# A transformer layer with attention and routed experts: routing and scatters moved among the first maxima, the sorted tiles closer together

## What is computed

```python
xn = _layernorm(x, axis=-1)                      # x: 8 x 256 x 128
x = x + attn(xn, Wqkv, bqkv, Wout, bout) + ffn(xn, ...)
# attn: 16 heads of 8 with rotary q and k
scores = jnp.einsum('bhtd,bhsd->bhts', q, k) / math.sqrt(D)
attn = jnp.einsum('bhts,bhsd->bhtd', jax.nn.softmax(scores, axis=-1), v)
# ffn: one shared expert, and the best 2 of 16
router_logits = jax.nn.sigmoid(x @ gate_w + gate_b)
expert_values, expert_indices = jax.lax.top_k(router_logits, k=2)
expert_values = expert_values / jnp.sum(expert_values, axis=-1, keepdims=True)
hg = jnp.einsum('bsd,edi->bsei', x, experts_wg)  # 128 -> 64
hu = jnp.einsum('bsd,edi->bsei', x, experts_wu)
all_outputs = jnp.einsum('bsei,eid->bsed', jax.nn.silu(hg) * hu, experts_wd)
# the two chosen, weighted; plus x and the shared expert
```

## Time and profile before

| | us |
|---|---|
| median of 3 runs | 302.07 (299.94 to 302.34) |
| the profiled execution, whole | 301.69 |
| its span, from first to last instruction | 299.9 |
| PE busy, share of the span | 213.9 (71%) |
| DVE busy | 150.9 (50%) |
| POOL busy | 143.9 (48%) |
| ACT busy | 127.6 (43%) |
| mean granted clock of PE | 0.869 of full speed |

### The profile page before, as it was taken

How to read it: one execution, slowest core, us unless ns; L and a number is a source line. 1 busy time by engine, 2 the same in 40 slices (tenths; PEclk the granted TensorE clock), 3 DMA queues, 4 the chain that set the end, 5 groups by cost and what they waited for, 6 DMA issues and landing times.

```text
span 299.9 us, 4752 instructions
## 1 busy us (share of the span) xinstructions
PE 213.9 (71%) x1603; PEld 131.2 (44%) x1603; DVE 150.9 (50%) x374; ACT 127.6 (43%) x292; POOL 143.9 (48%) x160
## 2 busy tenths in 40 slices
PE   0758965376868999139778789786978999996300
PEld 0326821162635545027545557474754446442200
DVE  6670199915494888213544365423526887710100
ACT  1365100002634676204544557644466776675000
POOL 9581048961347777780003370000000588888882
PEclk9995596757897999859999999979999999999555
DMA  7317689920325433152624142731225353333233
GB/s 254 52 39 209 179 213 271 276 83 0 107 72 152 111 107 108 52 136 72 183 82 109 43 117 74 205 97 37 87 77 156 97 97 41 39 39 70 36 70 87
DMA packets 50913, 32.48 MB, mean 108 GB/s; under 512 B 4542, under 2 KB 48830, under 8 KB 50622
## 3 DMA queue, kind: packets, MB, share of 16 engines
q1 hardware_dynamic: 43178, 26.40, 32.3%
q0 software_dynamic: 5632, 4.21, 8.0%
q10 hardware_dynamic: 2080, 1.57, 1.8%
HBM read 16.21 MB, written 15.77 MB: 107 GB/s over the span
## 4 chain that ended last, share of the span: by engine, by line
PE 42%; POOL 18%; issue 13%; ACT 8%; DVE 8%; DMA 7%; POOLq 1%; SPq 1%; ACTq 0%; DVEq 0%
POOL x_sorted L1054 10%; POOL resid L1071 8%; PE PV L600 7%; DMA q_hat<-mT 5%; PE S2a L586 4%; PE S2b L586 3%; PE Fa L515 2%; PE S1a L572 2%; PE Fc L483 2%; DVE mx L975 2%; PE S1b L572 2%; ACT ys L675 2%; PE Fb L467 2%; PE Fb L528 2%; PE Fa L528 2%
## 5 line engine op out<-in xcount | busy, mean ns | idle before, releaser
L1071 POOL DMA_INDIRECT resid<-y_sorted,slot_of x32 | 49.4, 1545 | 66.0 <-DMA y_sorted<-ys 56.5
L740 ACT ACTIVATE probs<-S2a 128x512 f32<-128x512 f32 x64 | 38.1, 596 | 62.8 <-PE S2a L586 62.6
L975 DVE TENSOR_REDUCE mx<-S1a 128x2 f32<-128x512 f32 x64 | 44.0, 687 | 41.5 <-PE S1a L572 40.9
L740 ACT ACTIVATE probs<-S2b 128x512 f32<-128x512 f32 x64 | 38.3, 598 | 49.2 <-PE S2b L586 48.8
L975 DVE TENSOR_REDUCE mx<-S1b 128x2 f32<-128x512 f32 x64 | 44.0, 688 | 8.9 <-PE S1b L572 8.2
L600 PE MATMUL PV<-probs,vx 128*32 128x256 f32 x512 | 41.6, 398 | 1.1 <-ACT probs L740 1.0
L586 PE MATMUL S2a<-q_hat,k_hat 102*128 102x256 bf16 x128 | 25.7, 283 | 19.7 <-DMA q_hat<-mT 18.6
L1054 POOL DMA_INDIRECT x_sorted<-xw,slot_of x32 | 31.8, 995 | 9.9 <-issue 8.5
L323 POOL TENSOR_TENSOR rope<-rope 128x256 f32<-128x256 f32 x14 | 10.2, 732 | 42.7 <-DVE rope L902 42.6
L572 PE MATMUL S1b<-k_hat,q_hat 96*128 96x256 bf16 x128 | 25.5, 281 | 5.2 <-DVE mx L975 5.2
L572 PE MATMUL S1a<-k_hat,q_hat 96*128 96x256 bf16 x128 | 26.2, 288 | 4.1 <-DVE mx L975 4.1
(11 more groups left out here) (197 smaller groups left out, 370.9 us busy)
## 6 DMA issues: line engine op xcount, KB each, us to landing
x_sorted<-ys SPq DMA_DIRECT2D x1, 3096.0 KB, 23.0
xs<-x_sorted SPq DMA_DIRECT2D x12, 258.0 KB, 3.1
q_hat<-q_parts SPq DMA_DIRECT2D x32, 96.0 KB, 2.3
y_sorted<-ys SPq DMA_DIRECT2D x12, 256.0 KB, 2.4
k_hat<-k_parts SPq DMA_DIRECT2D x28, 96.0 KB, 2.5
q_parts<-parts SPq DMA_DIRECT2D x8, 192.0 KB, 2.4
k_parts<-parts SPq DMA_DIRECT2D x7, 192.0 KB, 2.2
wgu_sb<-in_wgu SPq DMA_DIRECT2D x1, 1088.0 KB, 9.4
```

Source lines behind the costliest of these rows:

```text
L740: nc.scalar.activation(probs[:, head % (2 * NQ), :], S2[head % 2][:], ACT.Exp, scale=SCALE).then_inc(exp_done, 1)
L975: nc.vector.tensor_reduce(mx[:, (q // QB) % 2, (q // 2) % 2, :, q % 2, i], S1[i % 2][:].rearrange("p (t s) -> p t s", t=SB), axis=AX.X, op ...
L1071: nc.gpsimd.indirect_dma_start(resid[:, g, at, :], None, ys_dram, bass.IndirectOffsetOnAxis(ap=slot_of[:, t, k:k + 1], axis=0), compute_op ...
```

## The change

Seven edits, all in order and place but the last two:

- **Prologue.** `xw` of groups 1 to 3 on ACT, and DVE's variances for them, stand behind the split of batch 0. The zero fill of `x_sorted` goes from SP's queue to ACT's, as soon as group 0 has been loaded; `wgu`, `wd`, `wout` and `bout` go to ACT's queue behind V0.
- **Routing** starts at step -14 and does two stages a step, RANK stands in step -7, placement in steps -5 to -2, and POOL issues four scatters a block from block -1.
- **POOL.** Half-splits are set into other blocks (group 1, slot 1 into 2; group 2 into 5 and 10). `residual` goes from blocks -4, -1, 0, 1 to 11, 12, 13, 16. Group 2 is projected in blocks 2 and 3.
- **Sorted groups.** T of group `j` in step 46 + 5j//2, U two steps later, H seven, D ten. The buffer of loaded groups has seven places. The gathers stand from block 20 and still wait for all stores.
- **ACT** reads a step's items ahead of its exponential.
- **PE** loads a group's four register values with T, not with U.
- **Weights.** POOL multiplies the hidden values by the row's weight (`weigh`, in step 3 of a group); H waits for it. ACT's eviction of D is one plain copy.

```diff
-FIRST_SHARED, FIRST_SPARSE = 0, 10
-XRING = 6
+FIRST_SHARED, FIRST_SPARSE = 0, 46
+XRING = 7
...
-RESIDUAL_BLOCK = {-4: 0, -1: 1, 0: 2, 1: 3}
+RESIDUAL_BLOCK = {11: 0, 12: 1, 13: 2, 16: 3}
...
-ROUTE_STEP = -12
-PLACE_STEP = 1
-SORTED_LEAD, STORED_LAG = 6, 9
-SCATTER_BLOCK = 2
-SCATTERS = 5
-GATHER_BLOCK = 21
+ROUTE_STEP = -14
+PLACE_STEP = -5
+SORTED_LEAD, STORED_LAG = 5, 12
+SCATTER_BLOCK = -1
+SCATTERS = 4
+GATHER_BLOCK = 20
...
-        for kind, late in (("T", 0), ("U", 2), ("H", 5), ("D", 7)):
+        for kind, late in (("T", 0), ("U", 2), ("H", 7), ("D", 10)):
...
                 elif kind == "H":
-                    emptied(pe, ("U", n))
+                    if n < G:
+                        emptied(pe, ("U", n))
+                    else:
+                        pe.wait_ge(hid_weighed, n - G + 1)
...
+            act.wait_ge(ld_x[0], 16)
+            act.wait_ge(ys_zeroed, 1)
+            act.dma_start(xs_dram.rearrange("(p j) c -> p (j c)", p=P).rearrange("p (j c) -> p j c", c=ZERO),
...
-                    for t in range(QT):
-                        last = nc.scalar.activation(ys[:, j % OUTS, t, :], bank[:, t * C:(t + 1) * C], ACT.Copy,
-                                                    scale=xs[:, j % XRING, t, C:XW])
-                    last.then_inc(done, 1)
+                    nc.scalar.activation(ys[:, j % OUTS].rearrange("p t c -> p (t c)"), bank[:], ACT.Copy).then_inc(done, 1)
...
-                if 0 <= blk < NBLK:
-                    exponentials(blk * NQ + i)
...
                 for kind, n in items_before(blk, i):
                     read(kind, n)
+                if 0 <= blk < NBLK:
+                    exponentials(blk * NQ + i)
...
+            def weigh(j):
+
+                emptied(pool, ("U", G + j))
+                rows = hid[:, (G + j) % 2].rearrange("p (t i) -> p t i", i=I)
+                nc.gpsimd.tensor_tensor(rows, rows, xs[:, j % XRING, :, C:XW].broadcast_to([P, QT, I]),
+                                        ALU.mult).then_inc(hid_weighed, 1)
```

More of the change, by code:

```diff
@@ L496, in fill @@
                     j = n - G
+                    if j == 0:
+                        pe.wait_ge(owner_ready, 1)
+                    _, owners[n] = nc.values_load_multi_w_load_instructions(
+                        owner_at[0:1, QT * j:QT * (j + 1)], engines=[mybir.EngineType.PE], min_val=0, max_val=(E - 1) * P,
+                        skip_runtime_bounds_check_because="it is the least of a count and 15, times 128")
                     pe.wait_ge(xs_ld[j % XRING], 16 * (j // XRING + 1))
@@ L505, in fill @@
                     else:
-                        if n == G:
-                            pe.wait_ge(owner_ready, 1)
                         emptied(pe, ("T", n))
-                        _, owners[n] = nc.values_load_multi_w_load_instructions(
-                            owner_at[0:1, QT * (n - G):QT * (n - G + 1)], engines=[mybir.EngineType.PE],
-                            min_val=0, max_val=(E - 1) * P,
-                            skip_runtime_bounds_check_because="it is the least of a count and 15, times 128")
                         tiles, at = xsT[:, n % 2], owners[n]
@@ L715, in _ @@
                     act.dma_start(dram, parted).then_inc(scratch_done[0], 16)
-            read("X", 1)
-            normalise(3)
-            read("X", 2)
-            read("X", 3)
+            act.wait_ge(stats_ready, 2)
+            nc.scalar.activation(std[:, 1:], veps[:, 1:], ACT.Sqrt).then_inc(std_ready, 1)
+            for g in range(1, G):
+                normalise(g)
+            for g in range(1, G):
+                read("X", g)
             act.wait_ge(scratch_done[0], 16 * WRITES)
@@ L727, in _ @@
             read("V", 0)
+            act.dma_start(wgu_sb[:], wgu).then_inc(ld_up, 16)
+            act.wait_ge(wd_zeroed, 1)
+            for z in range(2):
+                act.dma_start(wd_sb[z][I * z:I * (z + 1), :], wd).then_inc(ld_down, 16)
+            act.dma_start(wout_sb[:], wout).then_inc(ld_wout, 16)
+            act.dma_start(bout_sb[:], bout.broadcast_to([P, C])).then_inc(ld_wout, 16)
             def halve_shared():
@@ L979, in _ @@
                     split_maxima(h, stage + 1)
[L980 to L983 removed]
+                for stage in range(ROUTE_STAGES):
+                    if ROUTE_STEP + stage // 2 == at:
+                        route(stage)
+                for stage in range(PLACE_STAGES):
+                    if PLACE_STEP + stage // 2 == at:
+                        place_rows(stage)
             for kind, n in EPILOGUE:
@@ L1076, in _ @@
                 split_batch(w, 0, 1)
-            for blk in range(FIRST, LAST + 1):
-                for (g, w, slot), at in SPLIT_BLOCK.items():
-                    if blk == at:
-                        split_batch(w, g, slot)
-                if blk in RESIDUAL_BLOCK:
-                    residual(RESIDUAL_BLOCK[blk])
-                first = SCATTERS * (blk - SCATTER_BLOCK)
-                for n in range(max(first, 0), min(first + SCATTERS, TOPK * NT)):
-                    scatter(n)
-                first = GATHERS * (blk - GATHER_BLOCK)
-                for p, k in gather_order()[max(first, 0):max(first + GATHERS, 0)]:
-                    gather(p, k)
+            for blk, i in steps():
+                if i == 0:
+                    for (g, w, slot), at in SPLIT_BLOCK.items():
+                        if blk == at:
+                            split_batch(w, g, slot)
+                    if blk in RESIDUAL_BLOCK:
+                        residual(RESIDUAL_BLOCK[blk])
+                    first = SCATTERS * (blk - SCATTER_BLOCK)
+                    for n in range(max(first, 0), min(first + SCATTERS, TOPK * NT)):
+                        scatter(n)
+                    first = GATHERS * (blk - GATHER_BLOCK)
+                    for p, k in gather_order()[max(first, 0):max(first + GATHERS, 0)]:
+                        gather(p, k)
+                for j in range(QUADS):
+                    if sparse_step(j) + 3 == 4 * blk + i:
+                        weigh(j)
     return nc
```

45 lines of the change are left out of this document (15 added, 30 removed), and 4 rows, old and new, of the table SPLIT_BLOCK.

## The result

The changed kernel takes 274.8 us (median of four, 274.3 to 275.31) where the kernel before takes 302.2 on the same chip: a ratio of 0.910 (95%: 0.903 to 0.916). I had said 287 and a range of 277 to 297.

A forecast was written before the change was run, and what follows sets the result against it. The run of gathers on POOL, waiting for the last sorted tile, ends the chain. First T at 135, 81.4 us to the last D, 4.1 to the first gather, then 64.4: 284.9, stated as 287 us; range 277 to 297.

The forecast's parts named there:

- The frame: End of the kernel: the time is when the last sorted tile is stored plus 64.4 us, gathers unchanged.
- the prologue's 5.3: Ahead of the first maximum: xw and variances now stand behind batch 0's split, making the prologue 5.3 us later.
- POOL's chain: POOL from the slots at 66.0: scatters 42.9, half-splits 19.2, first residual 2.5, ending at 130.6 and setting the pace.
- the new wait of DVE for the first residual: Step 42: DVE waits some 5 us for POOL's residual(0) before reading O1 of batch 1.
- the sorted stage: First T to last D: 75.7 us of PE work at 0.93 full, 81.4 us, ending at 216.4.
- The work: PE's work from first T to last D: 80.4, minus 2.8 for three steps, minus 1.9 for O1: 75.7 us.
- The fill: How full PE is in the sorted groups: 0.93, between 0.83 as before and 0.99 as without sorted tiles.
- My sum for the front: Steps ahead of the first T: step 0 at 68, then 54.9 us adjusted; step 42 at about 125 without POOL's wait.
- Rival 1: Front or sorted groups: prologue not late, 281.5 us, or PE at 0.99, 282; both 277. Chance 0.2.
- Rival 2: Sorted groups stay loose: fills bunched on three banks, PE 0.83, 90.9 us, 296.5 as a whole. Chance 0.22.
- Rival 3: Whole kernel: hardly any gain, 299 to 305; sorted groups loose and another 3 to 8 us lost in front. Chance 0.08.
- Rival 4: Sorted groups: H waits for POOL's multiplication, each group losing 1.5 us or more, time over 305. Chance 0.05.

The follow-up runs named there:

- the old front: The kernel before with ACT reading items first and the changed kernel's sorted stage; prologue, zero fill, routing, scatters, half-splits and residuals as before: 272.03 us, ratio 0.909.

## Why the prediction was right, and where it failed

- **The frame held.** "When the last tile is stored, plus 64.4": 64.3 to 64.5 us in every kernel timed. The span from last D to first gather was 4.1 by my sum and 3.8 in the trace.
- **Everything on the path up to the first T held** within 2 us: the prologue's 5.3 (5.0 at the first maximum; 4.1 there and 5.0 at the first T against the run with the old one), the slots, POOL's chain (64.5 us from the slots to the residual, 64.6 by my sum), and the new wait of DVE for the first residual, which the run with early residuals confirmed as on the path. That the first T stands within 0.2 us of 135 is luck: the residual came 1.5 us early, and T followed 5.7 us behind it where I had taken some 4.
- **The step that failed is the sorted stage, in both of its terms.** I wrote "PE's work: 80.4, minus three steps of 0.93 (2.8), minus O1 (1.9): 75.7", and then a fill of 0.93. The busy time was 69.2 and the fill 0.98. With the right busy time alone my sum gives 74.4 us, so 7.0 of the 10.9 us missed are work and 3.9 are fill.
- **The work.** The mis-sized term is the 80.4 from which the sum starts; what it takes off was sized well. O1 of batch 1, with its part of the shared expert, is 16 matmuls, and in the kernel before they run from 136.00 to the next item's start at 137.88, the 1.9 us that I took. The attention ahead of the last D fell by 20 PV matmuls (164 to 144) and 10 of the scores (161 to 151). From one start to the next, eight PV matmuls take 0.57 us and two of the scores 0.22 or 0.23 where PE is full, as in the changed kernel:

```profile
154.58 0.64 PE L593 MATMUL PV<-probs,vx 128*32 128x256 f32 x8
155.15 0.39 PE L579 MATMUL S2b<-q_hat,k_hat 102*128 102x256 bf16 x2
155.38 0.38 PE L565 MATMUL S1b<-k_hat,q_hat 96*128 96x256 bf16 x2
```

  That is 2.6 us, where I took 2.8. So an estimate of the 659 matmuls at this density is 69.2 + 1.9 + 2.6 = 73.7 us, and some 6.7 of the 80.4 were no work. One part comes from the holes: the two kernels with the same 645 matmuls differ by 3.7 us of busy time with 10.1 and 0.5 us of holes, and here there were 16.1. Another comes from the clock, 0.97 against 0.99 over the stage: V's eight matmuls took 430 ns on average before and 275 after. How the 6.7 divide between the two is not shown.
- **The fill.** I named the right waits and then took a value "above the middle". That the rows were `ys` and the register load misled me to treat three edits as equals. The load at T is worth 0, the short eviction about 3 us of the stage, and the order on ACT 13 to 17. The signs of the mechanism that I had named all came: PE 98% busy, no wait on `ys`, none of H on `hid`. Those that named a time did not: PE was to be busy to 216 and the first gather to start at 220, and it was 205 and 209.
- **What the prediction did not see at all:** the same order was holding up steps 0 to 7. By itself it brings the first scatter from 86.0 to 77.2 and the first T from 133.2 to 124.3. My sum for the front started from the 54.9 us of the earlier trace rows as if these were fixed by work. The sum for the front was right all the same, because there POOL's chain, not the steps, sets the time, and it absorbs any gain in the steps: step 0 came 5 us earlier than I had worked out, step 42 some 2, and DVE then waited the longer. The zero fill landed in 18.1 us (I had taken 23 as the worst case), and the first T lost nothing to it that can be seen.
- **So the attribution was wrong even where the numbers were right.** I expected a change of many small gains. In fact one edit gives some 25 us and the weights on POOL 3 to 4, and with these two alone the ratio is 0.905 (0.899 to 0.910) where the whole change has 0.910 (0.903 to 0.916), so the rest sums to nothing that can be told from noise. From ACT's order alone to the whole change, the first T moves 10.5 us **later** (8.7 of it are the prologue and the late residuals, by the run without both, which still stands 1.8 later), the stage gets 8.7 shorter (weights 3, batch 1's projection that now lies ahead of it 3, fewer steps 2), and 0.8 are gained behind it. (The projection ran from 127.1 to 130.0 in the kernel with ACT's order alone, with PE's matmuls at 377 ns there and not 275.)
- **Rival 1** ("the sorted stage fills as the plain one does", 0.99) is what happened, at 0.2; it gave 282 since it used the 75.7. **Rival 2** (fills bunched on three banks) fell: with four items in a step PE waits nowhere over 0.4 us. By the order of the lists such a step can't run with ACT's old order (not run), so the closer placement rests on the new one. **Rival 3** (hardly any gain) fell with the 27 us. **Rival 4** fell: POOL's multiplication takes 0.62 us (0.73 taken), and POOL waits 40.0 us in all for DVE's `hid`, while PE never waits for POOL in the stage.
- The Trainium skill (GPSIMD Engine Reference, Engine selection) would have kept the multiplication on VectorE, as POOL is about twice slower. The trace agrees on POOL being slower, 0.62 us against 0.42, that is 1.5 times. So POOL costs 0.2 us more an instruction; what the edit brings comes from ACT's eviction, 0.6 and not 1.15 us.

## What to carry to other kernels

When two in-order engines feed each other, read what an idle engine has **ready in front of it** but may not touch, because another instruction stands first. In this kernel the ACT order, seen as 1.14 us of idle time beside a full bank, was worth more than every moved scatter; let work that is ready stand ahead of work that waits for the partner. And don't subtract from a busy time taken with holes: count the instructions and price them from start to start in a stretch where they stand close.

A gain ahead of a chain of fixed length (here 32 scatters of 1.27 us each, and what stands between them) is lost unless the chain itself starts earlier and is left unbroken. What an early finish must then also get is an earlier place in the program: with POOL's scatters unbroken, T in step 34 and not 40 gave 7.7 us on one chip. (From step 46 to 40 T was moved only together with other edits.)

## What the runs showed of the hardware

**Busy time of PE grows with the holes.** 645 matmuls whose mean durations in the two traces agree within 6% in every group of four or more are 71.96 us busy when close and 75.67 with 10 us of holes, at clock 0.99 both times. Close matmuls overlap in the records: rows of two start 0.22 us apart and last 0.39. For the same reason the busy times of PE's groups can't be added up: in the stage of the changed kernel they sum to 96.6 us, where the engine is 69.2 busy.

**DVE's instructions can grow sevenfold beside POOL's.** `ends` takes 0.17 or 1.23 us, the longer time while POOL computes a residual from two tiles, and both end together (60.89 and 60.86). `hot` takes 1.55 us and not 0.69 with the early residuals alone. Not every instruction grows: DVE's maxima take 0.68 us in both traces. Which ones do was not tried apart.

**One chip lost 21 to 29 us to waits that no instruction explains** (21 with the old front, 23 in the kernel before, 29 with T in step 34, each against its time on another chip). In all four kernels profiled there, between 75 and 125 us, most of it while POOL scattered, ACT and DVE stood still for up to 12 us at a time and PE in three of them for up to 9, with no releasing instruction in the profile (it writes "issue" or "remote"). PE, DVE and ACT of the kernel with T in step 40:

```profile
91.59 0.59 PE L579 MATMUL S2a<-q_hat,k_hat 102*128 102x256 bf16 x2 [9.27 <-issue]
...
92.28 0.69 DVE L975 TENSOR_REDUCE mx<-S1a 128x2 f32<-128x512 f32 x1 [11.33 <-issue]
...
90.85 0.60 ACT L741 ACTIVATE probs<-S2a 128x512 f32<-128x512 f32 x1 [10.04 <-remote]
```

The stage behind it ran as elsewhere (72.1, 71.0, 71.4 and 73.3 us), and so did the gathers. In the traces from the other chips the same stretch has no such rows. What stops the engines there I can't say; it was not tried.
